# A fused attention and feed-forward layer on one core: products with V on two halves of the array's rows, and another order of the work

## The reference

```
Q, K = x Wq^T, x Wk^T          # 8 heads of 64
V    = x Wv^T                  # 8 heads of 128
P    = softmax(Q K^T)          # per head, 256 x 256, no scaling
x1   = layernorm(x + sum over heads of P V)
h    = silu(s1 * (x1 W1^T)) * (s2 * (x1 W2^T))     # 512 wide
h    = gelu(sh1 * (h H1^T)); h = gelu(sh2 * (h H2^T))
out  = layernorm(x1 + s3 * (h W3^T))
```

## Time and profile before

| what | value |
|---|---|
| time, median of 3 runs | 976.01 us (975.59 to 977.19) |
| the profiled execution's own time | 976.76 us |
| its span, first to last instruction | 974.9 us |
| mean granted TensorE clock | 0.995 |
| PE busy | 960.4 us (99%) |
| ACT busy | 881.8 us (90%) |
| DVE busy | 726.3 us (74%) |
| POOL busy | 589.4 us (60%) |
| chain that ended last, by engine | PE 96%, DVE 2%, issue 1%, POOL 1% |

### The profile page before, as it was taken

One profiled execution on the slowest core, in us unless ns is written; L12 is line 12 of the kernel. 1 busy time (PEld: TensorE's weight loads), 2 busy tenths in 40 slices (PEclk: granted clock), 3 DMA queues, 4 the chain that ended last, 5 costly groups with the idle time before them and its releaser, 6 DMA issues.

```text
span 974.9 us, 19735 instructions
## 1 busy us (share of the span) xinstructions
PE 960.4 (99%) x6573; PEld 819.3 (84%) x6573; DVE 726.3 (74%) x1653; ACT 881.8 (90%) x2108; POOL 589.4 (60%) x591
## 2 busy tenths in 40 slices
PE   8989999999999999999999999999999999999996
PEld 6878888888888888888888888888888888888886
DVE  7988677786777867777686777867778677777756
ACT  7968999999999999998999999999999999989964
POOL 6945655647565574656656666475665746566664
PEclk9999999999999999999999999999999999999998
DMA  6000000001000010000000000010000100000000
GB/s 198 9 24 2 18 6 12 23 2 34 1 12 23 1 33 2 15 20 12 23 1 23 13 11 23 2 33 1 12 23 1 34 1 12 12 8 16 1 12 23
DMA packets 22053, 17.81 MB, mean 18 GB/s; under 512 B 1088, under 2 KB 18496, under 8 KB 21952
## 3 DMA queue, kind: packets, MB, share of 16 engines
q1 hardware_dynamic: 21952, 16.53, 5.7%
HBM read 12.33 MB, written 4.19 MB: 17 GB/s over the span
## 4 chain that ended last, share of the span: by engine, by line
PE 96%; DVE 2%; issue 1%; POOL 1%; ACT 0%; DMA 0%; DVEq 0%; POOLq 0%; ACTq 0%
PE bank L1452 14%; PE bank L1446 13%; PE bank L1564 13%; PE bank L1565 13%; PE bank L1448 12%; PE bank L1447 12%; PE bank L1495 11%; PE bank L1544 3%; PE bank L1545 3%; PE bank L1624 1%; PE bank L1625 1%; PE bank L1950 0%; DVE t_lo L277 0%; DMA out_x<-y 0%; DVE y L1020 0%
## 5 line engine op out<-in xcount | busy, mean ns | idle before, releaser
L342 POOL TENSOR_TENSOR prob<-prob,inv_total 128x512 f32<-128x512 f32 x256 | 262.9, 1043 | 120.9 <-DVE inv_total L989 120.9
L559 ACT ACTIVATE prob<-bank,neg_max 128x256 f32<-128x256 f32 x512 | 238.9, 481 | 4.1 <-DVE neg_max L983 3.0
L277 DVE TENSOR_TENSOR pt_lo<-bank,pt_hi 128x512 fp32r<-128x512 f32 x256 | 175.5, 687 | 81.0 <-ACT pt_hi L280 80.9
L983 DVE TENSOR_REDUCE neg_max<-bank 128x2 f32<-128x512 f32 x256 | 169.8, 679 | 40.5 <-PE bank L1495 40.5
L280 ACT ACTIVATE pt_hi<-bank 128x512 fp32r<-128x512 f32 x256 | 154.0, 603 | 30.0 <-PE bank L1452 29.0
L1452 PE MATMUL bank<-ident,prob 128*128 128x128 f32 x1024 | 154.0, 274 | 2.1 <-issue 2.0
L1446 PE MATMUL bank<-pt_hi,v_hi 128*128 128x256 f32 x512 | 154.4, 302 | 0.0
L1452 PEld LDWEIGHTS bank<-ident,prob 128*128 128x128 f32 x1024 | 124.6, 141 | 29.5 <-issue 2.6
L1448 PE MATMUL bank<-pt_hi,v_lo 128*128 128x256 f32 x512 | 144.5, 282 | 0.0
L1447 PE MATMUL bank<-pt_lo,v_hi 128*128 128x256 f32 x512 | 144.2, 282 | 0.0
L277 POOL TENSOR_TENSOR odd_lo<-gelus,odd_hi 128x512 fp32r<-128x512 f32 (+1 forms) x62 | 78.7, 1282 | 63.4 <-ACT odd_hi L280 62.4
(11 more groups left out here) (134 smaller groups left out, 2402.7 us busy)
## 6 DMA issues: line engine op xcount, KB each, us to landing
xt_in<-in_x_t SPq DMA_DIRECT2D x16, 256.0 KB, 2.7
res<-in_x SPq DMA_DIRECT2D x16, 256.0 KB, 2.8
out_x<-y SPq DMA_DIRECT2D x15, 256.0 KB, 2.3
h_in<-in_h_t SPq DMA_DIRECT2D x2, 1024.0 KB, 9.2
w_in<-in_w_t SPq DMA_DIRECT2D x3, 256.0 KB, 5.8
wv_in<-in_wv_t SPq DMA_DIRECT2D x1, 512.0 KB, 4.7
out_x<-y SPq DMA_DIRECT2D x2, 128.0 KB, 1.8
wq_in<-in_wq_t SPq DMA_DIRECT2D x1, 192.0 KB, 3.5
```

The source lines that it names most:

```text
L277: return eng.tensor_tensor(dst, src, hi.bitcast(F32), ALU.subtract)
L342: nc.gpsimd.tensor_tensor(prob[:, s, :, :], prob[:, s, :, :], inv_total[:, u, :].unsqueeze(2).to_broadcast([P, NT, N]), ALU.mult).then_inc ...
L559: last = nc.scalar.activation(prob[:, slot(i, u, RING), nt, :], sc_bank(i, u)[:, nt * N:(nt + 1) * N], ACT.Exp, bias=neg_max[:, u, nt:nt + 1],
L983: nc.vector.tensor_reduce(neg_max[:, u, :], sc_bank(i, u).rearrange("p (t m) -> p t m", m=N), AX.X, ALU.max, negate=True).then_inc(s_max, 1)
```

## The change

The two halves of a product with V go to two banks where the unit stands in a list; elsewhere nothing changes in it. The list is `HALVES` (units 5, 6, 7, 9, 10, 11, 13 of a pair), with other lists for pairs 0, 1 and 15. Bank 6 becomes the second accumulator. ScalarE copies bank 7's part to `at`, and VectorE adds bank 6's (`acc_sum`); for a sequence without such units VectorE alone copies.

```
-        acc = bank[7]
+        acc = (bank[7], bank[6])
...
+HALVES = (5, 6, 7, 9, 10, 11, 13)
+HALVES_OTHER = {0: (5, 13), 1: (0, 1, 5, 6, 7, 9, 10, 11, 13), 15: (0, 2, 7)}
...
+        def by_halves(i, b):
+            return [u for u in HALVES_OTHER.get(i, HALVES) if u // H == b]
+        def in_two_banks(i, b):
+            return sum(bool(by_halves(*divmod(n, 2))) for n in range(2 * i + b))
...
             def acc_copy(i, b):
-                if there(i):
+                if there(i) and by_halves(i, b):
                     act.wait_ge(s_pv, after(i, J, (b + 1) * H))
                     need(act, s_at, after(i, 2, b))
-                    copy(at[:, :], acc[:, b * N:(b + 1) * N]).then_inc(s_acc, 1)
+                    copy(at[:, :], acc[0][:, of_batch(b)]).then_inc(s_accx, 1)
...
+            def acc_sum(i, b):
+                if there(i):
+                    m = of_batch(b)
+                    if by_halves(i, b):
+                        dve.wait_ge(s_accx, in_two_banks(i, b) + 1)
+                        nc.vector.tensor_tensor(at[:, :], acc[1][:, m], at[:, :], ALU.add).then_inc(s_acc, 1)
+                    else:
+                        dve.wait_ge(s_pv, after(i, J, (b + 1) * H))
+                        need(dve, s_at, after(i, 2, b))
+                        nc.vector.tensor_copy(at[:, :], acc[0][:, m]).then_inc(s_acc, 1)
...
-                    for mt in range(NT):
-                        v = slice(h * D, (h + 1) * D)
-                        last = three(acc[:, b * N:(b + 1) * N], v_hi[:, b * NT + mt, v], v_lo[:, b * NT + mt, v],
-                                     pt_hi[:, s, mt, :], pt_lo[:, s, mt, :],
-                                     h == 0 and mt == 0, h == H - 1 and mt == NT - 1)
+                    m, v = of_batch(b), slice(h * D, (h + 1) * D)
+                    halves = by_halves(i, b)
+                    if u in halves:
+                        for mt in range(NT):
+                            t = b * NT + mt
+                            for term, (left, right) in enumerate(((v_hi, pt_hi), (v_hi, pt_lo), (v_lo, pt_hi))):
+                                for n in range(2):
+                                    rows, units = slice(n * R, (n + 1) * R), halves if n else range(b * H, (b + 1) * H)
+                                    last = mm(acc[n][:, m], left[rows, t, v], right[rows, s, mt, :],
+                                              start=(u == units[0] and mt == 0 and term == 0),
+                                              stop=(u == units[-1] and mt == NT - 1 and term == 2))
+                    else:
+                        for mt in range(NT):
+                            last = three(acc[0][:, m], v_hi[:, b * NT + mt, v], v_lo[:, b * NT + mt, v],
+                                         pt_hi[:, s, mt, :], pt_lo[:, s, mt, :],
+                                         h == 0 and mt == 0, h == H - 1 and mt == NT - 1)
                     last.then_inc(s_pv, 1)
...
             for k in range(1, LAST):
+                load_xt(k + 2)
                 load_res(k)
-                load_xt(k + 2)
                 store(k - 2)
```

More of the change, by code:

```diff
@@ L711, in _ @@
+            pt_high(0, 4)
+            exp(0, 10)
+            t_high(1, 1)
+            exp(0, 11)
+            pt_high(0, 5)
+            t_high(1, 2)
+            weight_high(6)
+            weight_high(10)
+            v_high(0, 5)
             t_high(1, 3)
             exp(0, 12)
-            weight_high(10)
-            pt_high(0, 8)
+            pt_high(0, 6)
+            t_high(1, 4)
+            weight_high(8)
+            pt_high(0, 7)
             exp(0, 13)
             exp(0, 14)
+            v_high(0, 6)
@@ new lines, in _ @@
+                x1t_high(k - 1)
+                pt_high(k, 4)
+                gelu3(k - 2, 1)
+                pt_high(k, 5)
+                high(k - 2, 3, 1)
+                gelu3(k - 2, 2)
+                pt_high(k, 6)
+                tanh(k - 1, 0)
+                t_high(k + 1, 0)
+                pt_high(k, 7)
+                high(k - 2, 3, 2)
+                tanh(k - 1, 1)
+                gelu3(k - 2, 3)
+                high(k - 2, 3, 3)
+                exp(k, 10)
+                v_high(k, 4)
@@ L770, in _ @@
+                exp(k, 11)
+                pt_high(k, 8)
+                high(k - 1, 1, 0)
+                tanh(k - 1, 2)
+                yt_copy(k - 2)
+                high(k - 1, 1, 1)
+                v_high(k, 5)
+                exp(k, 12)
+                exp(k, 13)
+                exp(k, 14)
+                pt_high(k, 9)
+                tanh(k - 1, 3)
+                acc_copy(k, 0)
+                pt_high(k, 10)
+                v_high(k, 6)
+                exp(k, 15)
                 t_high(k + 1, 1)
@@ L800, in _ @@
+                pt_high(k, 12)
+                high(k - 1, 1, 3)
+                exp(k + 1, 0)
+                exp(k + 1, 1)
+                exp(k + 1, 2)
+                t_high(k + 1, 4)
+                t_high(k + 1, 5)
+                pt_high(k, 13)
+                exp(k + 1, 3)
                 gelu2(k - 1, 0)
+                t_high(k + 1, 6)
                 high(k - 1, 2, 0)
-                pt_high(k, 13)
+                t_high(k + 1, 7)
                 gelu2(k - 1, 1)
-                xt_high(k + 2)
@@ L1250, in _ @@
+                inverse(k, 7)
+                pt_low(k, 3)
+                norm1(k - 1, 1)
                 v_low(k, 2)
+                inverse(k, 8)
                 v_low(k, 3)
+                x1t_low(k - 1)
+                inverse(k, 9)
+                pt_low(k, 4)
+                pt_low(k, 5)
+                pt_low(k, 6)
+                silu(k - 1, 0)
+                t_low(k + 1, 0)
+                pt_low(k, 7)
+                row_max(k, 10)
+                row_max(k, 11)
+                silu(k - 1, 1)
@@ L1312, in _ @@
-                row_max(k + 1, 4)
-                stats1_of(k, 0)
-                row_max(k + 1, 5)
-                t_low(k + 1, 6)
-                norm1(k, 0)
+            row_max(15, 4)
+            pt_low(15, 0)
+            v_low(15, 1)
+            row_max(15, 5)
+            v_low(15, 2)
+            acc_sum(14, 1)
             res_add(14, 1)
-            t_low(15, 7)
+            inverse(15, 4)
             stats1_of(14, 1)
-            inverse(15, 3)
-            pt_low(15, 0)
+            pt_low(15, 1)
@@ L1348, in _ @@
+            row_max(15, 11)
+            v_low(15, 5)
+            pt_low(15, 7)
             silu(14, 2)
-            row_max(15, 10)
-            row_max(15, 11)
-            pt_low(15, 7)
-            v_low(15, 5)
+            pt_low(15, 8)
+            row_max(15, 12)
+            pt_low(15, 9)
+            acc_sum(15, 0)
+            inverse(15, 11)
+            gate(14, 2)
             silu(14, 3)
-            gate(14, 2)
-            pt_low(15, 8)
+            inverse(15, 12)
             gate(14, 3)
-            pt_low(15, 9)
@@ L1949, in _ @@
             for _ in range(WARM):
[L1950 removed]
+                mm(acc[0][:, 0:P], ident[:, :], ident[:, :], start=True, stop=True)
             query_or_key(0, 0)
```

1167 lines of the change are left out of this document (554 added, 613 removed).

## The result

The changed kernel takes 980.63 us (median of 6 runs, 977.98 to 982.27), the kernel before on the same chip 975.6 us (6 runs, 975.29 to 977.19): ratio 1.0045, 95% interval 1.0035 to 1.0056. It is 5 us slower where 5.5 us faster was forecast. The profiled execution has a span of 978.6 us and took 980.51.

What follows compares the result with a forecast made beforehand. The prediction took TensorE, busy for 99% of the span, as the bound: 4.7 us less from bursts and 0.8 from exits, all else 0, so 976.0 - 5.5 = 970.5 us, range 968.4 to 974.8.

Steps and rivals of the forecast that it cites:

- Bursts and exits: TensorE's half-row bursts: twelve fewer save 4.7 us, 17 more exits into transposes 0.8; 0.44 us in every cycle.
- The ledger: Check of TensorE's steps in a cycle: 57.1 us plus six bursts at 2.3 gives 59.4, trace 59.30.
- The products on half rows: V products on TensorE: 630 pairs replace 630 full matmuls at about the same step, taken as 0.
- rival 3: Long half-row bursts in the cycles run slower; 20 ns a pair make 10 us, 980.6; chance 0.06.
- rival 4: Score and V products side by side still pay the change: 22 us more, 998; chance 0.03 with the overhead.
- ScalarE, VectorE, and the short distances: Other engines' work lies beside TensorE's, and shortened producer-to-waiter distances in the cycles still fit; taken as 0.
- rival 1: Small waits inside the cycles, at T4 or qk2+, eat 1.4 to 5.6 us: 972 to 976; chance 0.15.
- rival 2: Accumulator's loop: TensorE waits before V0 each cycle for a late copy; 2.5 us late gives 986; chance 0.05.
- Rival 5: Better ends: the first waits get shorter, 968 us; chance 0.05.
- The ends: First and last parts: 8.3 us of waits in another order, net 0, with 2 us either way.
- The range: Whole kernel, 968.4 to 974.8 us: the forecast with 2 us of ends, and rival 1's larger part.
- the ends lose over 3 us: One of the signs, at the kernel's first and last parts, by which the prediction would count itself wrong.

Runs made afterwards that it cites:

- full_rows: The changed kernel with empty lists of half-row units, so every product with V runs on all rows: 983.14 us, ratio 1.0073 to the kernel before.
- pad32: The changed kernel with 32 never-executed instructions in TensorE's path not taken: 976.55 us, ratio 1.0005 to the kernel before.
- pad256: The changed kernel with 256 never-executed instructions, one whole block, in the path not taken: 982.18 us, ratio 1.0063 to the kernel before.
- halves_late: pad32 with VectorE's two small operations on the scales moved behind the sixth row maximum: 974.44 us, ratio 0.9984 to the kernel before.
- flag_late: halves_late with the flag's transpose and the second pair's last query/key product moved behind V10: 974.15 us, ratio 0.9989 to the kernel before.
- dve: The changed kernel with the fifth query/key product's low part moved ahead of VectorE's two operations on the scales: 980.74 us, ratio 1.0045 to the kernel before.
- before_pad212: The kernel before with 212 never-executed instructions in the branch not taken: 976.51 us, ratio 1.0012 to the kernel before.
- after_straight: The changed kernel without TensorE's choice of path, only the path taken standing straight on: 975.75 us, ratio 0.9986 to the kernel before.
- straight_both: halves_late with flag_late's two moves and without the choice of path: 973.44 us, ratio 0.9975 to the kernel before.
- after_fallthrough: The changed kernel with the choice turned round, so the path taken falls through and the other is jumped to: 976.0 us, ratio 0.9994 to the kernel before.

## Why the prediction was wrong

- *Bursts and exits, 5.5 us less.* Right. The cycle came out at 58.93 us, the way in and out at the prices given, and the half rows alone at 0.42 us a cycle, 6.6 us of 6.9 in all (full_rows against pad32). The ledger that backed it was a little less exact than it says: its terms as printed add up to 57.3, with the bursts 59.6, and only unrounded steps bring it near 59.4. What changes between the kernels does not hang on that.
- *The products on half rows, priced at 0.* Right, up to the thirtieth pair: rivals 3 and 4 fell. The Trainium skill, TensorEngine Tiling (Array Packing), section Instruction Overhead, would have had the 630 extra matmuls cost an estimated 16 us; TensorE's busy time fell by 0.5 us.
- *ScalarE, VectorE, and the short distances, priced at 0.* Right inside the cycles: not one wait between 87 and 941 us, so rivals 1 and 2 fell. Rival 5, better ends, fell with the next point.
- *The ends, "I see no net sum and take 0, with 2 us either way".* This step failed. The ends took 9.2 us. Three things make most of it. First, the code behind the branch: the changed lengths of both paths and of the first part moved the jump's target to the end of a block, and the second stop of 2.94 us, with the slow clock behind it, is worth 4.1 us (pad32) to 5.6 us (pad256 against pad32). In the table these are the 3.9 us at the branch and the 1.4 in cycle 1. Second, the first 15 us: the reorder put two 128x4 operations of VectorE beside GpSimd's first splits, ahead of what TensorE waits for; 2.1 us by the medians of halves_late and pad32, 0.7 to 1.4 by the table. Third, 1.4 us up to T13(0), mostly waits for ScalarE, which flag_late only moved, and 0.95 at T15(0) for GpSimd, which shows only where the branch's stop does not cover it.
- *The range.* "Or if the ends lose over 3 us" was the right test; but 2 us either way for them had no row behind it. The table's first column shows what should have been read: the ends of the kernel before lose 18.5 us in all (first column without the row of cycles 2 to 13), three times the gain that was forecast, and the first part was wholly reordered.

None of the rivals named the branch. The rows to see it by were in the trace of before: a 2.4 us stop that ends 2.7 us after a 16 KB fetch starts, and the next fetch just behind. The Trainium skill, Runtime: NRT & Kernel Launch, section Instruction fetch mechanics, says that code comes in blocks of 16 KB or 256 instructions, fetched ahead in sequence only, and that a branch out of them stalls; the traces agree (2.0 to 2.4 us for the first block).

**Open.** When the clock falls. The profiles of the changed kernel, pad256 and dve have 6.83 us at half speed behind the two stops, that of the kernel before 3.41 us behind one, that of before_pad212 none behind two. It also differs between runs of one kernel, and the spread of the times goes with it: of after_straight's runs the two at a mean clock of 0.997 and 0.998 took 972.36 and 972.74 us, the six at 0.996 took 973.87 to 975.99, the four at 0.994 took 975.98 to 976.23. A stretch of 3.41 us at half clock takes an estimated 0.002 off the mean and costs up to 1.7 us. So a part of what separates the medians above is how often a kernel meets such a stretch (all runs of straight_both are at 0.997 or 0.998), and what decides that no run shows. And what remains of the 5.5 us at the ends is placed but not recovered.

## What to carry to other kernels

Price a steady loop by its steps from one matmul to the next, and it can be forecast to 0.1 us in 59. But a gain of half a percent is as large as what the prologue loses, so each end of a reordered kernel needs its own sum, engine by engine. If code is added or removed near a jump, count instructions to the target's block end: the same program, 32 dead instructions longer, was 4 us faster. Before two medians are compared to a microsecond, look at the mean clock of their runs. And when a wait is found, move what holds the queue up, not the instruction that is late.

## What the runs showed of the hardware

- A taken jump stopped TensorE for 2.0 to 2.4 us, in nine kernels. It resumed 2.5 to 2.9 us after the 16 KB fetch of the target's block had started, and the fetch of the next block started 0.5 to 1.1 us after that. Where the target was at a block's end a second stop of 1.75 to 3.5 us followed, which ended 2.4 to 2.9 us after the start of that next fetch. A choice whose taken path falls through showed no stop.
- A 16 KB fetch of instructions beside a store of 128 KB made it land 1.4 us later (3.26 us against 1.80 to 1.82; after_fallthrough).
- An operation on 128x4 values took 1.13 to 1.19 us on VectorE beside a GpSimd subtraction (11.76 to 14.27 us in the changed kernel), and 0.16 us in the kernel before at 14.47, when GpSimd ran none. The Trainium skill, SBUF — State Buffer, section SBUF: two separate sides, says that a VectorE operation with two inputs in SBUF and a GpSimd operation exclude each other on a shared port; the low part, with one input in PSUM, took 0.68 us beside the same GpSimd work. The trace agrees: in dve the 128x4 operation (12.52 and 1.19 us) ended at 13.71, when GpSimd's subtractions (11.16 and 2.54) had ended.
- Thirty pairs of half-row matmuls on end, of two kinds and with other operands, keep a step of 0.120 us.
